# Turning the probabilities of every head on VectorE, and three small moves beside it

## The reference

```python
y = layernorm(x)
q, k = heads(y @ Wq), heads(y @ Wk)                # 8 heads, 64 columns each
wv = topk_mask(y @ Ws, 2) * sigmoid(y @ Ws)        # which 2 of 5 experts give the values
v = einsum('bthe,btek->bhtk', wv, einsum('btd,edk->btek', y, Wv))
probs = softmax(q @ k.T * 64 ** -0.5)              # 512 x 512 for each batch and head
attn = probs @ v
out = einsum('bthe,bthk,ekd->btd', topk_mask(y @ Wd, 2), attn, Wo)
x = x + tanh(g_ffn) * out
```

## Time and profile before

| | |
|---|---|
| median of 3 runs | 1174.29 us (1172.51 to 1174.52) |
| the profiled execution, its time | 1175.16 us |
| its span, first to last instruction | 1173.4 us |
| PE / PEld / DVE busy | 1128.9 / 855.5 / 915.4 us |
| ACT / POOL busy | 634.2 / 657.0 us |
| granted TensorE clock | 0.999 of full speed |

### The profile page before, as it was taken

The page is one execution under the profiler, slowest core; times in us unless marked ns, Lnnn a source line. Parts: engine busy times, 40 slices in busy tenths (PEclk is TensorE's granted clock), DMA queues, the critical chain, the costliest instruction groups (busy, mean ns, idle before and its releaser), DMA issues.

```text
span 1173.4 us, 19136 instructions
## 1 busy us (share of the span) xinstructions
PE 1128.9 (96%) x5885; PEld 855.5 (73%) x5885; DVE 915.4 (78%) x1656; ACT 634.2 (54%) x1332; POOL 657.0 (56%) x476
## 2 busy tenths in 40 slices
PE   7999999999999999999999999999999999999998
PEld 6788888888888888876767667667666666667655
DVE  7988887878787857476786886887887886976986
ACT  7634343434343433457566556556556565666654
POOL 2635242424242425439389298397497496595693
PEclk9999999999999999999999999999999999999999
DMA  5341414141414123422323324224233233231140
GB/s 199 143 135 45 135 46 133 46 132 47 132 49 130 57 86 115 148 89 72 90 55 109 88 54 138 59 63 151 54 89 107 54 110 104 52 122 48 47 126 37
DMA packets 76606, 108.44 MB, mean 92 GB/s; under 512 B 7712, under 2 KB 40224, under 8 KB 76576
## 3 DMA queue, kind: packets, MB, share of 16 engines
q1 hardware_dynamic: 76576, 108.07, 30.7%
HBM read 58.76 MB, written 16.78 MB: 64 GB/s over the span
## 4 chain that ended last, share of the span: by engine, by line
PE 71%; DVE 11%; ACT 7%; issue 7%; POOL 3%; DMA 1%; DVEq 0%; ACTq 0%
PE ps_f L992 22%; PE ps_o L2267 9%; PE ps_s L992 7%; PE ps_h L992 6%; PE ps_r L2193 6%; PE ps_r L2226 4%; PE ps_s L2244 4%; ACT probs_odd L1663 4%; PE ps_r L2202 3%; DVE nmax L1853 3%; PE ps_s L2252 3%; DVE z_tmp L1872 2%; ACT tmp L1663 1%; POOL spare L1580 1%; DVE z L1883 1%
## 5 line engine op out<-in xcount | busy, mean ns | idle before, releaser
L1853 DVE TENSOR_REDUCE nmax<-ps_s 128x1 f32<-128x512 f32 x256 | 158.4, 679 | 75.0 <-PE ps_s L2244 74.0
L1580 POOL TENSOR_TENSOR spare<-xv,pick 128x512 f32<-128x512 f32 x160 | 170.6, 1066 | 35.8 <-DVE pick L1968 22.9
L1598 POOL TENSOR_TENSOR z<-z,z_tmp 128x1280 f32<-128x1280 f32 x35 | 102.8, 2937 | 156.0 <-DVE z_tmp L1872 153.7
L1586 POOL TENSOR_TENSOR spare<-spare 128x512 f32<-128x512 f32 x128 | 180.5, 1410 | 10.0
L1663 ACT ACTIVATE probs_odd<-ps_s,nmax 128x512 f32<-128x512 f32 x124 | 146.7, 1183 | 0.0
L1663 ACT ACTIVATE tmp<-ps_s,nmax 128x512 f32<-128x512 f32 x124 | 85.6, 690 | 102.6 <-DVE nmax L1853 102.6
L2267 PE MATMUL ps_o<-pt,spare 128*64 128x512 f32 x496 | 115.0, 606 | 2.3 <-issue 2.3
L254 POOL TENSOR_TENSOR e_t<-e_t 128x512 fp32r<-128x512 f32 x28 | 35.4, 1302 | 135.8 <-ACT e_t L510 135.8
L2244 PE MATMUL ps_s<-k,q 64*128 64x512 f32 x768 | 106.5, 408 | 0.9 <-ACT pt L1672 0.9
L2244 PEld LDWEIGHTS ps_s<-k,q 64*128 64x128 f32 x768 | 67.4, 184 | 46.9 <-issue 34.3
L2252 PE MATMUL ps_s<-ident,probs_odd 128*128 128x128 f32 x512 | 77.4, 279 | 19.6 <-ACT probs_odd L1663 17.9
(11 more groups left out here) (245 smaller groups left out, 2302.0 us busy)
## 6 DMA issues: line engine op xcount, KB each, us to landing
pt<-tmp SPq DMA_DIRECT2D x248, 128.0 KB, 2.6
stage<-in_x SPq DMA_DIRECT2D x32, 256.0 KB, 3.1
x_sb<-in_x SPq DMA_DIRECT2D x8, 1024.0 KB, 5.3
x_dram<-x_sb SPq DMA_DIRECT2D x32, 256.0 KB, 3.2
stage<-x_dram SPq DMA_DIRECT2D x8, 1024.0 KB, 5.5
x_sb<-x_dram SPq DMA_DIRECT2D x8, 1024.0 KB, 5.5
out_dram<-x_sb SPq DMA_DIRECT2D x31, 256.0 KB, 2.6
stage<-in_ctx_t SPq DMA_DIRECT2D x28, 256.0 KB, 2.8
```

The lines of the kernel that those rows point to most:

```text
L1580: pool.tensor_tensor(v_tmp[:] if e else acc, xv[:, :, e, :].unsqueeze(2).broadcast_to(shape), pick[:, e, :, 2 * p:2 * p + 2].unsqueeze(3). ...
L1586: pool.tensor_tensor(acc, acc, v_tmp[:], ALU.add).then_inc(v_steps, 1)
L1598: pool.tensor_tensor(zv, zv, z_tmp[:, h % 2], ALU.add).then_inc(z_pool, 1)
L1853: dve.tensor_reduce(nmax[:, n:n + 1], ps_s[:, n % BANKS, :], AX_X, ALU.max, negate=True).then_inc(nmax_ready, 1)
```

## The change

All tiles now go the way of the even ones, except in the last two rounds of the last batch. The odd tile's transposes on TensorE and its copy on ScalarE are gone, and a bank is free when its exponential is done (`p_exp`). The probabilities of a round lie together in 2048 columns, round by round in `tmp` and a new buffer `late`, which lies behind and partly over the second half of `spare`. In them each run of 64 columns holds two row tiles of one head, and one VectorE instruction turns both: two instructions of 1024 columns a round in place of two of 512. Each of the four moves of a round carries 512 columns a partition piece in place of 256. The mask is laid out by head, tile and expert, as `coefficients` reads it. The copy of the norm values is made by ScalarE in `normalise`. The exponentials of the last two rounds write contiguously and read the scores in another order.

```diff
-        mask = sb("mask", [P, E, NT, H], BF16)
+        mask = sb("mask", [P, H, NT, E], BF16)
...
-        probs_odd = sb("probs_odd", [P, BANKS // 2, T])
+        probs = both.tmp[:].rearrange("p k t -> p (k t)"), both.late
...
+        def blocks(n):
+            return probs[n // BANKS % 2].rearrange("p (j i s a) -> p j i s a", i=2, s=2, a=BLOCK)[:, :, n % 2,
+                                                                                              n % BANKS // 2, :]
...
+        def plainly(columns):
+            return columns.rearrange("p (k a q) -> p k a q", q=QUADS, a=BLOCK)
+
+        def scores_by_keys(columns):
+            return columns.rearrange("p (q k a) -> p k a q", q=QUADS, a=BLOCK)
...
                 for q in range(QUADS):
-                    sp.dma_start(by_rows(2 * p % 4)[:, r % 2, q].rearrange("p k s a -> p (k s a)"),
-                                 probs_even[q * BLOCK:(q + 1) * BLOCK, r % 2].rearrange(
-                                     "p (j k) s a -> p j (k s a)", j=QUADS)).then_inc(moved[r % 2], 16)
+                    sp.dma_start(by_rows(p)[:, r % 2, q].rearrange("p k i s a -> p (k i s a)"),
+                                 probs[r % 2][q * BLOCK:(q + 1) * BLOCK].rearrange(
+                                     "p (j u) -> p j u", j=QUADS)).then_inc(moved[r % 2], 16)
...
             def normalise(b, tiles):
+                if tiles[0] == 0:
+                    act.wait_ge(last_newton, ROOT_STEPS + 1)
+                    act.activation(norm[:], x1_norm[:, :, bass.ds(b * NT, NT)], ACT.Copy).then_inc(norm_ready, 1)
+                act.wait_ge(x1_loaded, b * 16)
                 act.wait_ge(norm_ready, b)
-                act.wait_ge(x1_loaded, b * 16)
...
-                act.activation(turned(n), scored(n), ACT.Copy).then_inc(pt_ready, 1)
...
-                act.activation(by_keys(plain_probs(n)), by_scores(ps_s[:, n % BANKS, :]), ACT.Exp, bias=nmax[:, n:n + 1],
+                act.activation(plainly(plain_probs(n)), scores_by_keys(ps_s[:, n % BANKS, :]), ACT.Exp, bias=nmax[:, n:n + 1],
...
-                dve.tensor_scalar(norm[:], x1_norm[:, :, bass.ds(b * NT, NT)], 1.0, None, ALU.mult).then_inc(norm_ready, 1)
...
-            def turn_blocks(b, n):
-
-                dve.wait_ge(p_exp, b * STEPS + n + 1)
-                dve.transpose(even_probs(n), even_probs(n)).then_inc(blocks_turned, 1)
+            def turn_blocks(b, r, i):
+
+                dve.wait_ge(p_exp, b * STEPS + r * BANKS + i + 3)
+                both_tiles = probs[r % 2].rearrange("p (j i u) -> p j i u", i=2, u=2 * BLOCK)[:, :, i, :]
+                dve.transpose(both_tiles, both_tiles).then_inc(blocks_turned, 2)
...
-                    pe.wait_ge(pt_ready, odd_turned(b, n + 1 - BANKS))
+                    pe.wait_ge(p_exp, b * STEPS + n + 2 - BANKS)
...
-                    elif place == TURNS:
-                        for tile in range(n * BANKS + 1, n * BANKS + BANKS, 2):
-                            turn_probs(b, tile)
```

More of the change, by code:

```diff
@@ L87 @@
     spare: object
+    late: object
     tmp: object
@@ L1651, in scores_exp @@
                 h, t = head_tile(n)
[L1652 to L1671, removed]
-                act.activation(turned(n), scored(n), ACT.Copy).then_inc(pt_ready, 1)
+                if n % BANKS == 0 and (n >= 2 * BANKS or not first):
+                    act.wait_ge(moved[n // BANKS % 2], (b * PAIRS + n // PAIR) * MOVED)
+                act.activation(blocks(n), ps_s[:, n % BANKS, :].rearrange("p (j a) -> p j a", a=BLOCK), ACT.Exp,
+                               bias=nmax[:, n:n + 1], accum_out=den[:, h, t:t + 1]).then_inc(p_exp, 1)
             def last_exp(b, n):
@@ L1895, in coefficients @@
                     dve.wait_ge(mask_ready, b + 1)
-                dve.tensor_tensor(coef[:, heads], mask[:, :, :, heads].rearrange("p e t h -> p h t e"),
+                dve.tensor_tensor(coef[:, heads], mask[:, heads],
                                   rden[:, heads, :].unsqueeze(3).broadcast_to([P, 2, NT, E]),
@@ L1972, in route_values @@
                     dve.wait_ge(coef_ready, b * PAIRS)
-                dve.tensor_scalar(mask[:].rearrange("p e t h -> p e (t h)"), logits[:, 1], 1.5, None,
+                dve.tensor_scalar(mask[:].rearrange("p h t e -> p e t h"),
+                                  logits[:, 1].rearrange("p e (t h) -> p e t h", h=H), 1.5, None,
                                   ALU.is_lt).then_inc(mask_ready, 1)
@@ L1978, in step @@
                 if place == SCORES:
-                    if n == NORMALISE_AT and not first:
-                        take_norm(b)
                     for p in range(PAIRS):
@@ L2000, in step @@
                     if 0 <= n < ROUNDS:
-                        for tile in range(n * BANKS, n * BANKS + BANKS, 2):
-                            turn_blocks(b, tile)
+                        for i in range(2):
+                            turn_blocks(b, n, i)
                     if n == LAST_SUMS_AT[0]:
@@ L2265, in values @@
                     for a in range(2):
-                        rows = by_rows(p % 2 * 2 + a)[:, :, :, k].rearrange("p r q s a -> p q r (s a)")
+                        rows = by_rows(p)[:, :, :, k, a].rearrange("p r q s a -> p q r (s a)")
                         end = pe.matmul(ps_o[head_rows(a), :], v_acc[:, p, k, a, :], rows, start=k == 0,
@@ L2292, in values_half @@
                     for a in range(2):
-                        rows = by_rows(p % 2 * 2 + a)[:, half, :, k].rearrange("p q s a -> p q (s a)")
+                        rows = by_rows(p)[:, half, :, k, a].rearrange("p q s a -> p q (s a)")
                         end = pe.matmul(out[head_rows(a)], v_acc[:, p, k, a, :], rows, start=k == 0, stop=k == NT - 1)
```

42 lines of the change are left out of this document (12 added, 30 removed).

## The result

The changed kernel takes 1190.45 us (median of 4 runs, 1188.33 to 1190.89), the kernel before 1173.4 us in the same series. The ratio (of the means of the two sets of runs) is 1.0142, 95% interval 1.0124 to 1.0159: slower by 1.4%. The forecast was 1174.5 us with a range of 1162 to 1184; the prediction was wrong.

What follows compares the result with a forecast made beforehand. TensorE was taken to bound one stretch of each pass and VectorE, after the change, the other: 35.9 + 46.55 + 1.5 clock loss = 83.95 us against 84.0. With first rounds -0.5 and tail +0.6: 1174.5 us, range 1162 to 1184.

Steps and rivals of the forecast that it cites:

- A: Stretch of a pass (rounds S5 to S12) from S8 scores to first `turn_z` of S11: forecast 35.9 us, 1.65 longer.
- The wide turn: VectorE's 1024-column turn, two a round: forecast 1.22 us each, 1.06 us more per round, 8.5 us per pass.
- the S10 scores: Round in the first stretch: TensorE forecast to wait some 3 us for the low part of `k` 1 from VectorE.
- `turn_z` in S11: End of the first stretch: TensorE forecast to wait some 5.6 us for VectorE's sum of the last head into `z`.
- B: Rest of a pass, from `turn_z` of S11 to the next S8 scores, still set by TensorE: forecast 46.55 us from 49.75.
- three signs that were to show the prediction wrong: A short wait in S11, a clock that holds, or a wide turn far from 1.22 us.
- the size of the clock loss: Slow TensorE work behind the S11 wait in each pass: forecast 1.5 us, bounds 0 and 3.0.
- the low clock outlasts the first work: Rival: the spell behind the S11 wait costs 3.0 us, a pass 85.45, the kernel 1184.5 us; chance 0.16.
- the tail: End of the last batch: doubled moves of round 5 cost +1.9, plain exponentials give back about 1.3; forecast +0.6 us.
- The clock holds: Rival: no clock loss behind the waits, or it is hidden; a pass 82.45 us, the kernel 1163.5 us; chance 0.24.
- TensorE still sets the end: Rival: VectorE's late work has slack, so all 12.1 us a pass go; the kernel 1089 us; chance 0.05.
- The wide turn saves nothing: Rival: it takes 1.37 us like two narrow turns, or stalls against GpSimd; the kernel 1181 us; chance 0.07.

Runs made afterwards that it cites:

- experiment 1: Changed kernel plus unread filler matmuls on TensorE in front of both long waits of each pass: 1171.91 us, ratio 0.9982 to the kernel before.
- experiment 8: Kernel before with only the mask laid out by head, tile and expert: 1169.49 us, ratio 0.9963.
- experiment 11: Changed kernel with the moves of round 5 of the last batch issued before the residual load: 1188.87 us, ratio 1.0128 to the kernel before.
- experiment 4: Changed kernel with VectorE's turn covering only 128 of 1024 columns, output not the reference's: 1144.39 us, ratio 0.9744 to the kernel before.
- experiments 5 and 12: Changed kernel with odd tiles of pairs 0 and 1 back on TensorE and ScalarE: 1154.12 us; with round 5's moves also ahead of the residual load: 1152.64 us.
- experiment 9: Kernel before with the mask written three times in its old layout, as a delay on VectorE: 1169.78 us, ratio 0.9961.

## Why the prediction was wrong, point by point

**Most of the mechanism was right.** VectorE's chain sets A. The wide turn was taken as 1.22 us and measures 1.22 (median 1217 ns over 124). TensorE's waits come where they were put: 3.5 us before the S10 scores (forecast some 3), 3.7 to 5.1 before `turn_z` in S11 (forecast 5.6), each released as said. Without a clock loss a pass is 82.60 us (experiment 1); the forecast's terms for A and B give 82.45. None of the three signs that were to show the prediction wrong came: the S11 wait is long, the clock falls, and the turn has the forecast length. (The sums took 84.0 us for a pass before. The S8 scores of the next pass start at 910.16 and not at the 910.26 where the earlier trace rows end, and the pass is 83.85; this shifts both sides by 0.1 us and the difference by nothing.)

`coef` in S7 stayed at 1.86 us with the new layout, here and in experiment 8. GpSimd's sums run from 821.09 us, so the `coef` of 822.23 lies beside them. The Trainium skill's page SBUF — State Buffer (section "Who interferes with whom") says that a VectorE instruction with two SBUF inputs contends with a GpSimd instruction that reads SBUF. The rows agree: beside no GpSimd sum the same product takes 0.19 us (830.67).

**The step that failed is the size of the clock loss.** I took 1.5 us a pass with bounds 0 and 3.0; it is 2.6, inside the bounds, and above the point of 1.9 from which the rival "the low clock outlasts the first work" was to decide. So the pass is that of this rival, 85.45 us (measured 85.22), but not for its reason: it let the low clock cover the next scores too, and those last 1.66 or 1.67 us behind all seven spells, which is full clock. Its number was luck. Against experiment 1 (A 36.30, `turn_z` to the next scores 5.04, the rest of B 41.26) the mean of six passes divides so:

- *The S11 wait.* From `turn_z` to the next scores the kernel after needs 7.31 and 6.68 us in the two kinds of pass, without loss 5.04: 1.85 us on the mean in place of 1.5. I had taken part of the spell as harmless because its matmuls are short transposes. But `turn_z` itself lasts 2.82 us for 1.47.
- *The S10 wait.* I put its loss into TensorE's own slack, that is, at nothing. That slack is not free: the slow matmuls are products whose result VectorE needs. In the slow pass VectorE waits 0.97 us for ScalarE's part of `q` (854.33), and ScalarE 2.03 us for the product (L2166) behind it, and A is 37.4 us in place of 36.2 (742.54 to 778.71). The mean of A is 36.76 us, +0.46.
- *The rest of B.* It is 41.9 us in place of 41.3 in every second pass, behind an A with the slow S10: +0.31 on the mean. `turn_z` comes at another time against GpSimd's work, `coef` in S5 lasts 1.29 us where it took 0.50, and TensorE waits longer for `es_t`:

```profile
802.51 0.50 DVE L1870 TENSOR_TENSOR coef<-mask,rden 128x40 f32<-128x40 bf16 x1
811.50 4.61 PE L2175 MATMUL ps_r<-c,es_t 128*128 128x400 f32 x24 [1.00 <-DVE es_t L1880]
887.85 1.29 DVE L1870 TENSOR_TENSOR coef<-mask,rden 128x40 f32<-128x40 bf16 x1
897.43 4.60 PE L2175 MATMUL ps_r<-c,es_t 128*128 128x400 f32 x24 [1.60 <-DVE es_t L1880]
```

1.85 + 0.46 + 0.31 = 2.62 us. The last of the three comes with the slow clock but is not TensorE's time; that the later `coef` makes the wait is read from the rows and was not tried. In six passes the kernel is 8.2 us slower where the forecast had it 0.3 us faster, and the seventh spell adds 0.7 us to what was forecast there.

**The second step that failed is the tail,** +3.7 us for +0.6. From the S5 scores to `values` 2 it was 14.09 us before (1127.04 to 1141.13) and is 19.19 after (1136.40 to 1155.59), +5.1, where I had +1.9. The rows show it (the first is of the kernel before; compare):

```profile
1127.04 1.66 PE L2244 MATMUL ps_s<-k,q 64*128 64x512 f32 x12
...
1136.40 1.66 PE L2217 MATMUL ps_s<-k,q 64*128 64x512 f32 x12
...
1146.63 0.40 SPq L1496 DMA_DIRECT2D x_sb<-x_dram  x1
1147.08 2.93 SPq L1511 DMA_DIRECT2D pt<-spare_late  x4
...
1155.59 5.29 PE L2239 MATMUL ps_o<-pt,spare_late 128*64 128x512 f32 x16 [8.43 <-issue]
```

The same four moves from issue to landing, in the kernel before, the changed one and that of experiment 11:

```profile
DMA to landing us min/median/max: 2.5/2.6/2.8
DMA to landing us min/median/max: 6.1/6.2/6.3
DMA to landing us min/median/max: 3.7/4.7/5.5
```

The moves start 1.4 us later after the scores than before, their issue takes 0.3 us longer, and they take 3.6 us more to land. The page of the profile gives the median of all moves as 4.5 to 4.6 us for 256 KB and 2.6 for 128 KB. So 2.0 us of the 3.6 are the size of the move: I had counted its issue and not its landing. The other 1.6 us fit the load of the residual, 1 MB, which is now issued 0.45 us before the moves and was issued 4.5 us before them; without it ahead (experiment 11) the landing is 1.5 us shorter. The other term was right: from `values` 2 to the end it is 30.91 us after and 32.27 before, 1.4 us less for a forecast 1.3.

**The last 3 us are the executions.** The forecast took the profiled run of before as 0.9 us above its median. The profiled run of after is 2.1 us below its median. This is the scatter of the executions and no step of the kernel.

**The small edits.** The norm copy does nothing that the runs can tell from noise, as forecast (0.22 us on ScalarE, taken as 0.3). The mask edit was priced at nothing and gives 0.4% alone, between 4 and 5 us, by phase and not by the layout. How much of that is in the changed kernel was not tried; its sums into `z` take 2.34 and 2.13 us, or 2.07 and 2.26 in every second pass, against 1.77 and 2.02 in experiment 8, so it is not on the good side of it.

**Rivals.** "The clock holds" is what experiment 1 made by force; its pass of 82.45 us stands there at 82.60. Its kernel time of 1163.5 us does not: 1171.91 was measured, with 4.1 us more than before from the last `turn_z` to the end. "TensorE still sets the end" is refuted: even with a turn of 0.29 us (experiment 4) the pass is 78.1 to 80.8 us, and waits for VectorE and GpSimd and the fallen clock remain. "The wide turn saves nothing" is refuted by its duration.

## What to carry to other kernels

Cut a loop at the points where engines meet and ask of each stretch which engine sets it; move work only in the stretches where the giver is the bound, as experiments 5 and 12 do, which turn 1.4% slower into 1.9% faster. A TensorE wait that an edit opens can cost more than its length: price the slow work behind it, and ask who waits for the results of that work before calling it slack. Two waits in one pass are one question, since filling one made the other longer. In a tail, count a transfer to its landing, with what its queue issues before it.

## What the runs showed of the hardware

- Behind waits of 3.5 to 5.3 us before `turn_z` the work up to the next scores took 6.3 to 7.9 us in place of 5.04, 1.3 to 2.9 us more, with a granted clock of 0.68 and 0.74 over it in the kernel after. Behind S10 waits of 3.5 to 3.7 us, where the clock fell to 1.2 GHz, 12 matmuls took up to 2.93 us for 1.66.
- The length of the wait does not decide it alone. After the same wait of 3.53 us the clock stayed at 2.4 GHz in every second pass of the kernel after, but fell in five passes running in experiment 11. After 2.2 us it fell in four of seven passes in experiment 4, and after 1.95 us it stayed. What decides is open.
- A mask write of 160 columns in bf16 with a stride takes 0.85 to 0.87 us, in order 0.24.
- A turn of 32x32 blocks in fp32 takes 0.29 us for 128 columns, 0.69 for 512 and 1.22 for 1024.
- A delay of some 0.6 us on VectorE in each pass made the kernel 0.4% faster, some 4.4 us (experiment 9), by moving GpSimd's work against VectorE's: a sum of 1280 columns lasts 1.77 us in some phases and 2.36 in others, and where it is short a GpSimd product beside it lasts 2.18 us in place of 1.05.
